# Causal mask of the turned attention scores: key-block rows in the stacks and zeroing on GpSimd, in place of mask products on TensorE

## The chip, the core and the metric

The kernel runs on one core of one Trainium2 chip. The core has TensorE (PE, matrix products; PEld is its weight load), VectorE (DVE), ScalarE (ACT), GpSimd (POOL), SyncE (SP, whose queue issues most DMAs), an on-chip memory of 128 partitions (SBUF) and eight accumulation banks (PSUM) that TensorE writes. Every engine works through its own queue in order, and the queues meet at semaphores. The metric is the time of one execution on the device in microseconds (us); lower is better.

## The reference

A transformer piece on x of shape 4 x 256 x 512 in fp32: causal attention with ALiBi, then a routed feed-forward (two of three experts), a gated MLP with a top-k cut, and the routed feed-forward again. The change lies in the attention:

```python
scores = jnp.einsum('bqhd,bkhd->bhqk', q, k) * SCALE      # 32 heads of 16, 4 batches of 256 tokens
rel = pos[None, :] - pos[:, None]
bias = slopes[:, None, None] * rel[None, :, :]
causal = rel <= 0
scores = jnp.where(causal[None, None], scores + bias[None], -jnp.inf)
attn = jax.nn.softmax(scores, axis=-1)
out = jnp.einsum('bhqk,bkhd->bqhd', attn, v).reshape(B, S, HIDDEN)
```

## The kernel before

**Stacks.** For every head, `qst` and `kst` hold queries and keys along partitions in bf16 parts: 96 rows of terms of q and k (`TROWS`), 8 rows of ALiBi parts (to `SROWS` = 104) and, for the turned scores alone, 3 rows that carry minus the maximum of each query (to `MROWS` = 107). One product of a stack of keys with a stack of queries so gives scores with bias, less the maximum.

**Stages.** Each of the four batches (b = 0 to 3) goes through projections, then scores with queries on partitions (`scores`, for the maxima that DVE reduces), then `attend`. In `attend` the scores are made again turned, with keys on partitions, in NG = 8 groups of G = 4 heads. The next batch's projections are woven into the score stage. After batch 3 come the feed-forward, the MLP and the second feed-forward, which the change leaves as they are.

**One group of `attend`, on each engine.** PE: `scores_t` (L1729 to L1749) writes three banks of slot g % 2. It first multiplies the identity with the mask `maskT` (L1737: 512 columns, L1740: twice 256), which puts -1e30 above the diagonal of the two square key/query tiles, and adds eight score products (L1744: 128 columns, L1746: 256 columns). ACT takes exp of all 1536 columns into `probsT` (L795), two buffers. PE `weigh` (L1756, L1761) multiplies the exponentials with the values. DVE copies the product out (`outT`, L1101), PE `back` (L1769) turns it, DVE divides (`normalise`: L1091, L1095, writes `o_tok`). `weigh(b, n)` waits for the exponentials of group n, and for `normalise` of group n-2, whose bank it takes. PE's order in step g is scores_t(g), weigh(g-1), back(g-2).

**What else stands on DVE's and POOL's queues in `attend`.** DVE: statistics of a normalisation (L1141) after groups 0 and 1, gate logits (`logit_row`, L1149, one after most groups of batches 1 and 2), the layer norm statistics of batch b+2 after group 3 (`ln_moments_of`) and its rows after group 5 (`ln_rows`, L1020), both for b < 2. In batch 3: three weight splits `w_first_lo` (L1351) ahead of group 0, and router steps of 4 to 14 tiny instructions after groups 2, 3, 5 and 6; ACT's exp of the router (L843) stands behind exp(3) and waits for the step after group 2. POOL: `norm_rstd` (L667, L670, L673) twice, and `ln` (L651, L653), on which DVE's `ln_rows` waits.

## Time and profile before

| | us |
|---|---|
| median of 3 runs (lowest, highest) | 714.89 (714.68, 716.71) |
| the profiled execution's own time | 714.72 |
| its span | 713.0 |
| PE busy in the span | 658.1 (92%) |
| DVE busy | 476.4 (67%) |
| ACT busy | 343.3 (48%) |
| POOL busy | 84.7 (12%) |
| exp L795, 32 of them | 46.2 busy, mean 1450 ns |

Starts are counted from the span's start. Matmuls overlap in PE's pipeline, so what a matmul costs is the distance to the next one's start, not its own duration. An entry in brackets behind a row is the idle time of the engine ahead of it and what ended it. The attend stages start at 68.2, 122.7, 178.2 and 225.7 us.

### The profile page before, as it was taken

The numbers are of one execution on the slowest core, as the hardware profiler recorded it, in microseconds if no ns is written. First come the engines' busy times: TensorE is split into PE (matmuls) and PEld (weight loads), VectorE is DVE, ScalarE is ACT, GpSimd is POOL, SyncE is SP. The second block draws the span as 40 slices with busy tenths as digits, with TensorE's granted clock in tenths as the row PEclk, the third lists the DMA queues.
The fourth block names the chain that finished last, engine by engine and source line by source line (L and its number), as shares of the span: only waits on it lengthen the run. The fifth ranks groups of instructions, "written<-read, shape, count | busy, mean of one in ns | idle before, by whom it ended". The sixth has DMA issues, their size and how long they took to land.

```text
span 713.0 us, 10154 instructions
## 1 busy us (share of the span) xinstructions
PE 658.1 (92%) x3784; PEld 486.1 (68%) x3784; DVE 476.4 (67%) x905; ACT 343.3 (48%) x536; POOL 84.7 (12%) x185
## 2 busy tenths in 40 slices
PE   5895999999998889999989999999999999999997
PEld 4783678678676567887776665756757555787875
DVE  6555495696589769787694655274463797868555
ACT  5221734613634663442357996485582924435221
POOL 4411002102100020100133000100100120100000
PEclk9987999999999999999999999999999999999999
DMA  8494423321744240000143000000001304000000
GB/s 269 123 276 123 116 63 89 94 90 56 236 124 151 106 151 9 0 1 1 25 169 126 0 1 0 1 0 1 0 1 42 136 0 177 2 29 16 16 30 30
DMA packets 31763, 51.35 MB, mean 72 GB/s; under 512 B 3433, under 2 KB 17132, under 8 KB 30159
## 3 DMA queue, kind: packets, MB, share of 16 engines
q1 hardware_dynamic: 31330, 49.12, 21.4%
q10 hardware_dynamic: 384, 1.57, 1.0%
q8 instruction: 31, 0.51, 0.3%
q14 instruction: 18, 0.15, 0.1%
HBM read 42.09 MB, written 8.40 MB: 71 GB/s over the span
## 4 chain that ended last, share of the span: by engine, by line
PE 76%; DVE 13%; ACT 4%; DMA 2%; issue 2%; POOL 1%; SPq 1%; ACTq 1%; DVEq 0%; POOLq 0%
PE ps L1815 12%; PE ps L1848 11%; PE ps L2040 11%; PE ps L1979 10%; PE ps L1678 6%; PE ps L1983 5%; PE ps L1756 2%; DVE nmax L1072 2%; PE ps L1746 2%; PE ps L1660 2%; PE ps L1824 2%; PE ps L1694 2%; DVE prodT L1587 1%; ACT sign_junk L966 1%; DVE x_sb L1416 1%
## 5 line engine op out<-in xcount | busy, mean ns | idle before, releaser
L2040 PE MATMUL ps<-wdT,prodT 128*128 128x512 f32 (+1 forms) x176 | 77.7, 597 | 0.4
L795 ACT ACTIVATE probsT<-ps 128x1536 f32<-128x1536 f32 x32 | 46.2, 1450 | 38.2 <-PE ps L1746 38.0
L2040 PEld LDWEIGHTS ps<-wdT,prodT 128*128 128x128 f32 (+1 forms) x176 | 32.8, 190 | 40.7 <-issue 38.3
L834 ACT ACTIVATE funs<-ps 128x512 f32<-128x512 f32 x16 | 9.6, 598 | 91.8 <-PE ps L1817 80.9
L667 POOL TENSOR_SCALAR ln_spread<-ln_moments 128x1 f32<-128x1 f32 x24 | 8.5, 354 | 298.4 <-DVE ln_moments L1143 298.3
L1149 DVE SCALAR_TENSOR_TENSOR junk<-x_sb,gate_row 128x512 f32<-128x512 f32 x48 | 41.2, 859 | 1.0
L1587 DVE COPY prodT<-ps 128x512 f32<-128x512 f32 (+1 forms) x24 | 13.7, 599 | 40.4 <-PE ps L2029 40.0
L1072 DVE TENSOR_REDUCE nmax<-ps 128x4 f32<-128x1024 f32 x32 | 38.8, 1213 | 0.0
L1416 DVE SCALAR_TENSOR_TENSOR x_sb<-b_row,coef,x_sb 128x512 f32<-128x512 f32 x48 | 36.2, 754 | 1.8
L901 ACT CAST aT_hi<-ps 128x512 fp32r<-128x512 f32 x32 | 17.2, 590 | 38.1 <-PE ps L1824 38.1
L966 ACT ACTIVATE sign_junk<-mlp_size_next,minus_guess 128x1376 bf16<-128x1376 f32 x24 | 34.6, 1443 | 0.8
L966 ACT ACTIVATE sign_junk<-mlp_size_main,minus_guess 128x1376 bf16<-128x1376 f32 x24 | 34.6, 1442 | 0.8
L1101 DVE COPY outT<-ps 128x256 f32<-128x256 f32 x32 | 13.5, 423 | 29.3 <-PE ps L1761 29.2
L660 POOL TENSOR_TENSOR parts<-resid,parts 128x512 bf16<-128x512 f32 x16 | 18.6, 1173 | 95.8 <-ACT parts L774 95.8
L1345 DVE TENSOR_TENSOR aT_lo<-ps,aT_hi 128x512 fp32r<-128x512 f32 x32 | 20.6, 685 | 12.8 <-ACT aT_hi L901 12.7
L1678 PE MATMUL ps<-rowsT_hi,wqkv_hi 128*128 128x256 f32 x128 | 23.6, 311 | 5.1 <-DVE rowsT_lo L1026 4.4
L1059 DVE SCALAR_TENSOR_TENSOR resid<-ps,qk_bias,parts 128x256 f32<-128x256 f32 x32 | 14.0, 479 | 18.3 <-ACT parts L767 18.3
L767 ACT ACTIVATE parts<-ps,qk_bias 128x256 bf16<-128x256 f32 x32 | 13.4, 468 | 26.7 <-PE ps L1678 26.6
L1425 DVE TENSOR_TENSOR x_sb<-ps,x_sb 128x512 f32<-128x512 f32 x16 | 11.0, 691 | 21.7 <-PE ps L1848 21.6
L1746 PE MATMUL ps<-qst,kst 107*128 107x256 bf16 x128 | 25.4, 278 | 0.0
L1717 PE MATMUL ps<-kst,qst 104*128 104x256 bf16 x128 | 24.5, 272 | 0.0
L1756 PE MATMUL ps<-probsT,v_ones 128*32 128x256 f32 x256 | 20.4, 391 | 3.9 <-DVE o_tok L1095 2.8
(280 smaller groups left out, 1720.5 us busy)
## 6 DMA issues: line engine op xcount, KB each, us to landing
cuts<-parts SPq DMA_DIRECT2D x16, 384.0 KB, 3.2
qst<-cuts SPq DMA_DIRECT2D x48, 128.0 KB, 2.7
w_first_raw<-in_L_ffn_w SPq DMA_DIRECT2D x6, 1024.0 KB, 8.0
w_second_raw<-in_L_ffn_w SPq DMA_DIRECT2D x6, 1024.0 KB, 8.6
kst<-cuts SPq DMA_DIRECT2D x36, 128.0 KB, 2.6
wqkv_raw<-in_L_attn_a_w_attn SPq DMA_DIRECT2D x3, 1024.0 KB, 8.2
wdT<-in_L_attn_b_w_down SPq DMA_DIRECT2D x1, 2560.0 KB, 10.0
wg_raw<-in_L_attn_b_w_gate SPq DMA_DIRECT2D x1, 2048.0 KB, 8.1
```

Of the source, the lines that this page charges most:

```text
L795: nc.scalar.activation(probsT[:, g % 2, :].rearrange("p (k n) -> p k n", k=3), slot[g % 2], ACT.Exp).then_inc(exp_ok.sem, 1)
L966: nc.scalar.activation(sign_junk[:, :], size_rows(n)[1][:, :], ACT.Sign, bias=minus_guess[:, i:i + 1], accum_out=probe_sum[:, i:i + 1]).th ...
L1072: nc.vector.tensor_reduce(nmax[:, 1, g * G:(g + 1) * G], sl[:, 1:3, :].rearrange("p s (h k) -> p (s h) k", h=2), AX.X, ALU.max, negate=Tru ...
L1149: nc.vector.scalar_tensor_tensor(out=junk[:, :], in0=x_sb[:, t, :], scalar=1.0, in1=gate_v[:, 0:D, e], op0=ALU.mult, op1=ALU.mult, accum_o ...
L1416: nc.vector.scalar_tensor_tensor(out=x, in0=b2_row[:, e, :], scalar=coef[:, n, e:e + 1], in1=x, op0=ALU.mult, op1=ALU.add).then_inc(ffn.b2 ...
L1678: last = nc.tensor.matmul(turn_bank(b, f)[:, m * S:(m + 1) * S], weight[:, side, c, columns], rows[:, c, :], start=(i == 0 and c == 0), st ...
L1746: m = nc.tensor.matmul(sl[:, 1 + i // 2, (i % 2) * S:(i % 2 + 1) * S], kst[0:MROWS, h, 0:P], qst[0:MROWS, h, :], start=False, stop=True, s ...
L1815: nc.tensor.matmul(ps[:, 2 * i + s, :], a[:, i, c, :], part[:, e, c, :], start=(k == 0 and c == 0), stop=False)
L1848: last = nc.tensor.matmul(ps[:, Y_BANK, :], a[:, s, c, :], part[:, e[s], c, :], start=(k == 0 and c == 0), stop=(k == len(products) - 1 an ...
L1979: last = nc.tensor.matmul(ps[:, first_bank + q, :], a[:, c, :], part[:, c, at_q], start=(k == 0 and c == 0), stop=(k == 2 and c == KC - 1))
L1983: last = nc.tensor.matmul(ps[:, first_bank + q, 0:IT], row_whole[:, c, :], end[:, c, :], start=(c == 0), stop=(c == KC - 1))
L2040: last = nc.tensor.matmul(ps[:, Y_BANK, :], prodT[0:m, c, :], wdT[0:m, c, :], start=(c == 0), stop=(c == IC - 1))
```

## The change

`maskT` and its three products are gone. The stacks get 15 more rows (`AROWS` = 122) for the turned scores: on the key side row i holds -1e30 for keys in a block of 16 behind block i, on the query side 1 for queries of block i. That masks keys of later blocks. Keys of the query's own block that lie behind the query are left, and POOL sets their exponentials to zero: `blank` does two `affine_select` per group, on 128 x 512 fp32 each, once exp has written them. `weigh` waits for POOL's count instead of ACT's, stands one group later in PE's order, and `probsT` has three buffers. The twice-per-batch `norm_rstd` and `ln` on POOL move behind groups 3, 4 and 6 of `blank`. Two DMAs bring the new rows (15 rows of 16 KB per stack) in the first stage. `h_sb`, `rowsT_lo` and `qk_bias` change places in SBUF.

```diff
 def alibi_rows(H, S):
...
+    q_rows += [0 * one] * MAX_PARTS
+    block = np.arange(S) // BLOCK
+    for i in range(S // BLOCK - 1):
+        k_rows.append(np.broadcast_to(bf16_parts(np.where(block > i, NEG, 0.0), 1)[0], (H, S)))
+        q_rows.append(np.broadcast_to(bf16_parts(np.where(block == i, 1.0, 0.0), 1)[0], (H, S)))
...
-        probsT = sb("probsT", [P, 2, 3 * D], F32)
+        probsT = sb("probsT", [P, 3, 3 * D], F32)
...
             gather(0, 1, (0,))
+            sp.dma_start(kst[MROWS:AROWS, :, :].bitcast(U16), k_alibi[MROWS - TROWS:]).then_inc(blocks_in, 16)
+            sp.dma_start(qst[MROWS:AROWS, :, :].bitcast(U16), q_alibi[MROWS - TROWS:]).then_inc(blocks_in, 16)
             sp.dma_start(x_sb[:, 2 * TB:T, :], x_v[:, 2 * TB:T, :]).then_inc(x_rest, 16)
...
+            def blank(b, between):
+
+                for g in range(NG):
+                    need(pool, exp_ok, b, g + 1)
+                    late = probsT[:, g % 3, 0:D].rearrange("p (h t) -> p h t", h=G)
+                    early = probsT[:, g % 3, D:].rearrange("p (h t) -> p h t", h=G)[:, :, 0:P]
+                    for weights in (early, late):
+                        nc.gpsimd.affine_select(out=weights, in_=weights, compare_op=ALU.is_ge, fill=0.0, base=0,
+                                                pattern=[[0, G], [1, P]], channel_multiplier=-1
+                                                ).then_inc(causal.sem, 1)
+                    between(g)
...
+            def small(b, g):
+                if b >= 1 and g in (3, 4):
+                    norm_rstd(norm2, (b - 1) * TB + g - 3)
+                if b + 2 < B and g == 6:
+                    ln(b + 2)
+
             for b in range(B - 1):
                 cut(b + 1)
-                if b >= 1:
-                    for j in range(TB):
-                        norm_rstd(norm2, (b - 1) * TB + j)
-                if b + 2 < B:
-                    ln(b + 2)
+                blank(b, lambda g: small(b, g))
             scale_route(norm2, route1, 0)
-            for t in range((B - 2) * TB, T):
+            blank(B - 1, lambda g: small(B - 1, g))
+            for t in range((B - 1) * TB, T):
                 norm_rstd(norm2, t)
...
-                    if g >= 2:
-                        need(act, pv_ps, b, g - 1)
-                    nc.scalar.activation(probsT[:, g % 2, :].rearrange("p (k n) -> p k n", k=3), slot[g % 2],
+                    if g >= 3:
+                        need(act, pv_ps, b, g - 2)
+                    nc.scalar.activation(probsT[:, g % 3, :].rearrange("p (k n) -> p k n", k=3), slot[g % 2],
...
-                nc.tensor.matmul(sl[:, 0, :].rearrange("p (h k) -> p h k", h=G), ident16[:, :], diagonal(maskT, G),
-                                 start=True, stop=False, skip_group_check=True)
-                for s in range(2):
-                    nc.tensor.matmul(sl[:, 1 + s, :].rearrange("p (h k) -> p h k", h=2)[:, :, 0:P], ident16[:, :],
-                                     diagonal(maskT, 2), start=True, stop=False, skip_group_check=True)
...
             def weigh(b, g):
-                need(pe, exp_ok, b, g + 1)
+                need(pe, causal, b, 2 * (g + 1))
...
-                for g in range(NG + 2):
+                for g in range(NG + 3):
                     if g < NG:
                         scores_t(b, g)
                     if g == 0 and 1 <= b < B - 1:
                         project_heads(b - 1, 1)
-                    if 1 <= g <= NG:
-                        n = g - 1
+                    if g == NG + 1 and b < B - 1:
+                        scores(b + 1, 0)
+                    if 2 <= g <= NG + 1:
+                        n = g - 2
...
                         weigh(b, n)
-                    if g == NG + 1 and b < B - 1:
-                        scores(b + 1, 0)
-                    if g >= 2:
-                        back(b, g - 2)
+                    if g >= 3:
+                        back(b, g - 3)
```

PE's queue in a middle group of batch 0, before. `ps` is PSUM; the first two lines are the mask products, L1744 and L1746 the score products (three more such pairs follow), L1756 and L1761 `weigh`, L1769 `back`.

```order
L1737 MATMUL ps<-maskT,ident_51 128x512 [waits exp_ok]
L1740 MATMUL ps<-maskT,ident_51 128x2x128 x2
L1744 MATMUL ps<-qst,kst 128x128
L1746 MATMUL ps<-qst,kst 128x256
...
L1756 MATMUL ps<-probsT,v_ones 32x256 [waits exp_ok,norm_ok]
L1756 MATMUL ps<-probsT,v_ones 32x256 x3
L1761 MATMUL ps<-probsT,v_ones 32x128 x4
L1769 MATMUL ps<-ident,outT 128x128 [waits outT_ok]
```

The same place in the changed kernel, whose line numbers are higher (L1760 and L1762 are the score products, L1772 and L1777 `weigh`, L1785 `back`):

```order
L1760 MATMUL ps<-qst,kst 128x128 [waits exp_ok]
L1762 MATMUL ps<-qst,kst 128x256
...
L1772 MATMUL ps<-probsT,v_ones 32x256 [waits causal,norm_ok]
L1772 MATMUL ps<-probsT,v_ones 32x256 x3
L1777 MATMUL ps<-probsT,v_ones 32x128 x4
L1785 MATMUL ps<-ident,outT 128x128 [waits outT_ok]
```

Three instructions are gone, and `weigh` waits for `causal`, which POOL raises, where it waited for `exp_ok`.

POOL's queue from the cuts of batches 0 and 1 (L660) over `ln` (L651, L653) to the first `norm_rstd`, in batch 1's attend stage, before:

```order
L660 TENSOR_TENSOR parts<-resid,parts 128x512 [waits part2] x8
L651 TENSOR_SCALAR spread<-moments 128x2 [waits stat]
L653 TENSOR_TENSOR rstd<-spread,neg_half 128x2 [waits rstd_ok]
L660 TENSOR_TENSOR parts<-resid,parts 128x512 [waits part2] x4
L667 TENSOR_SCALAR ln_spread<-ln_moments 128x1 [waits norm_stat]
L670 TENSOR_TENSOR ln_rstd<-ln_spread,neg_half 128x1 [waits norm_rstd]
L673 TENSOR_SCALAR ln_shift<-ln_moments,ln_rstd 128x1 [waits norm_rstd]
```

The changed kernel around group 3 of batch 1 (L677 is `affine_select`; `norm_rstd` is now L685, L688, L691):

```order
L677 AFFINE_SELECT probsT<-probsT 128x4x128 [waits exp_ok]
L677 AFFINE_SELECT probsT<-probsT 128x512
L685 TENSOR_SCALAR ln_spread<-ln_moments 128x1 [waits norm_stat]
L688 TENSOR_TENSOR ln_rstd<-ln_spread,neg_half 128x1 [waits norm_rstd]
L691 TENSOR_SCALAR ln_shift<-ln_moments,ln_rstd 128x1 [waits norm_rstd]
L677 AFFINE_SELECT probsT<-probsT 128x4x128 [waits exp_ok]
L677 AFFINE_SELECT probsT<-probsT 128x512
```

The three instructions of `norm_rstd` stood on a queue that nothing on PE waited for; now they stand between two groups' selects.

## Rows read from the trace of the kernel before

**Rows 1.** The page: span, and granted TensorE clock in 40 slices, in tenths.

```profile
span 713.0 us, 10154 instructions
...
PEclk9987999999999999999999999999999999999999
```

**Rows 2.** Timeline of PE, one group of batch 1: start, us, engine, line, operation.

```profile
131.04 0.38 PE L1737 MATMUL ps<-maskT,ident 128*128 128x512 bf16 x1
...
131.48 0.22 PE L1744 MATMUL ps<-qst,kst 107*128 107x128 bf16 x1
...
132.23 0.64 PE L1756 MATMUL ps<-probsT,v_ones 128*32 128x256 f32 x8
...
133.02 0.44 PE L1769 MATMUL ps<-ident,outT 128*128 128x128 f32 x2
133.30 0.38 PE L1737 MATMUL ps<-maskT,ident 128*128 128x512 bf16 x1
```

**Rows 3.** Timeline of ACT and DVE beside that group.

```profile
132.34 1.45 ACT L795 ACTIVATE probsT<-ps 128x1536 f32<-128x1536 f32 x1 [0.80 <-PE ps L1746]
...
133.16 0.42 DVE L1101 COPY outT<-ps 128x256 f32<-128x256 f32 x1 [0.56 <-PE ps L1761]
...
133.95 0.85 DVE L1149 SCALAR_TENSOR_TENSOR junk<-x_sb,gate_row 128x512 f32<-128x512 f32 x1
```

**Rows 4.** Timeline of PE, the end of batch 0's attend stage.

```profile
86.29 0.44 PE L1769 MATMUL ps<-ident,outT 128*128 128x128 f32 x2
87.35 0.64 PE L1756 MATMUL ps<-probsT,v_ones 128*32 128x256 f32 x8 [0.62 <-DVE o_tok L1095]
```

**Rows 5.** Timeline of POOL: selects and their nearest kin, and one `norm_rstd`.

```profile
8.96 0.95 POOL L630 MEMSET v_ones<- 128x1024 f32 x1
...
11.66 0.29 POOL L634 TENSOR_SCALAR_AFFINE_SELECT maskS<-maskS 128x128 bf16<-128x128 bf16 x1
...
12.66 0.45 POOL L643 TENSOR_TENSOR text<-ones,vision 128x128 f32<-128x128 f32 x1
...
111.01 1.16 POOL L660 TENSOR_TENSOR parts<-resid,parts 128x512 bf16<-128x512 f32 x1 [27.89 <-ACT parts L774]
...
130.25 0.23 POOL L667 TENSOR_SCALAR ln_spread<-ln_moments 128x1 f32<-128x1 f32 x1 [8.12 <-DVE ln_moments L1143]
...
131.24 0.27 POOL L673 TENSOR_SCALAR ln_shift<-ln_moments,ln_rstd 128x1 f32<-128x1 f32 x1
```

**Rows 6.** Timeline of POOL ahead of the MLP.

```profile
372.49 1.73 POOL L716 TENSOR_TENSOR hT_lo<-hT_all,hT_hi 128x512 fp32r<-128x512 f32 x1 [5.43 <-ACT hT_all L941]
374.18 2.28 POOL L716 TENSOR_TENSOR hT_lo_third<-hT_all_third,hT_hi_third 128x512 fp32r<-128x512 f32 x1
```

**Rows 7.** Timeline of DVE in the same stretch, and just behind it.

```profile
373.10 2.21 DVE L1600 TENSOR_TENSOR wu_lo<-wu_raw,wu_hi 128x1024 fp32r<-128x1024 f32 x1
...
377.05 1.22 DVE L1600 TENSOR_TENSOR wu_lo<-wu_raw,wu_hi 128x1024 fp32r<-128x1024 f32 x1
```

**Rows 8.** Timeline: attend of batch 0, first product and first of the next stage.

```profile
68.24 0.61 PE L1737 MATMUL ps<-maskT,ident 128*128 128x512 bf16 x1 [3.84 <-DMA qst<-nmaxT]
...
89.65 1.17 PE L1660 MATMUL ps<-wqkv_hi,rowsT_hi 128*128 128x512 f32 x4
```

**Rows 9.** Timeline: attend of batch 1, PE's first product, DVE's first reduction behind it.

```profile
122.67 0.39 PE L1737 MATMUL ps<-maskT,ident 128*128 128x512 bf16 x1 [1.42 <-DMA qst<-nmaxT]
...
147.79 0.69 DVE L1069 TENSOR_REDUCE nmax<-ps 128x4 f32<-128x512 f32 x1
```

**Rows 10.** Timeline: attend of batch 3, PE, DVE and ACT.

```profile
225.74 0.39 PE L1737 MATMUL ps<-maskT,ident 128*128 128x512 bf16 x1 [0.75 <-DMA qst<-nmaxT]
...
247.70 1.09 PE L1685 MATMUL ps<-ident,o_tok 128*128 128x128 f32 x8 [1.18 <-DVE o_tok L1095]
...
227.07 2.28 DVE L1351 TENSOR_TENSOR w_first_lo<-w_first_raw,w_first_hi 128x2048 fp32r<-128x2048 f32 x1
...
236.28 0.21 ACT L843 ACTIVATE tiny<-tiny 128x12 f32<-128x12 f32 x1 [1.84 <-DVE tiny L1283]
```

More of the change, by code:

```diff
@@ L25 @@
 MAX_PARTS = 3
+BLOCK = 16
 FIRST_GUESS = 0.78
@@ L181, in build @@
     MROWS = SROWS + MAX_PARTS
+    AROWS = MROWS + S // BLOCK - 1
     SCALE = 1.0 / HD
@@ L281, in build @@
         wqkv_lo = sb("wqkv_lo", [P, 3, KC, D], F32R, wqkv_at)
-        qk_bias = sb("qk_bias", [P, 2, HT], F32)
-        at[0] = wqkv_at + 3 * 4 * KC * D + 4 * TB * 2 * D
+        h_sb = sb("h_sb", [P, TB, D], F32)
+        rowsT_lo = sb("rowsT_lo", [P, KC, S], F32R)
         parts = sb("parts", [P, 2, 2, 3, HT // 2, S], BF16)
@@ L302, in build @@
         maskS = sb("maskS", [P, P], BF16)
-        maskT = sb("maskT", [P, P], BF16)
+        qk_bias = sb("qk_bias", [P, 2, HT], F32)
         nmax = sb("nmax", [P, TB, H], F32)
@@ L307, in build @@
         nmaxT = sb("nmaxT", [P, S], BF16)
-        h_sb = sb("h_sb", [P, TB, D], F32)
         stats = sb("stats", [P, TB, 6], F32)
@@ L389, in build @@
         wqkv_in = [sem(f"wqkv_in{n}") for n in range(3)]
-        wproj_in, alibi_in, bias_in = sem("wproj_in"), sem("alibi_in"), sem("bias_in")
+        wproj_in, alibi_in, blocks_in, bias_in = sem("wproj_in"), sem("alibi_in"), sem("blocks_in"), sem("bias_in")
         consts, ident_ok, bits_set = sem("consts"), sem("ident_ok"), sem("bits_set")
@@ L421, in build @@
         exp_ok = sig("exp_ok", NG)
+        causal = sig("causal", 2 * NG)
         pv_ps = sig("pv_ps", NG)
@@ L526, in _ @@
             sp.dma_start(bias_v[:, :], b_attn[2 * D:3 * D].partition_broadcast(P)).then_inc(bias_v_in, 16)
-            sp.dma_start(kst[TROWS:MROWS, :, :].bitcast(U16), k_alibi).then_inc(alibi_in, 16)
-            sp.dma_start(qst[TROWS:SROWS, :, :].bitcast(U16), q_alibi).then_inc(alibi_in, 16)
+            sp.dma_start(kst[TROWS:MROWS, :, :].bitcast(U16), k_alibi[0:MROWS - TROWS]).then_inc(alibi_in, 16)
+            sp.dma_start(qst[TROWS:SROWS, :, :].bitcast(U16), q_alibi[0:SROWS - TROWS]).then_inc(alibi_in, 16)
             sp.wait_ge(bias_cut, 4)
@@ L622, in constants @@
                 nc.gpsimd.memset(maskS[:, :], 0.0).then_inc(consts, 1)
-                nc.gpsimd.memset(maskT[:, :], 0.0).then_inc(consts, 1)
                 nc.gpsimd.memset(vision[:, :], 1.0).then_inc(consts, 1)
@@ L632, in constants @@
                 nc.gpsimd.tensor_copy(ident16[:, :], ident[:, :]).then_inc(consts, 1)
-                pool.wait_ge(consts, 5)
+                pool.wait_ge(consts, 4)
                 nc.gpsimd.affine_select(out=maskS[:, :], in_=maskS[:, :], compare_op=ALU.is_ge, fill=NEG,
                                         base=0, pattern=[[-1, P]], channel_multiplier=1).then_inc(consts, 1)
-                nc.gpsimd.affine_select(out=maskT[:, :], in_=maskT[:, :], compare_op=ALU.is_ge, fill=NEG,
-                                        base=0, pattern=[[1, P]], channel_multiplier=-1).then_inc(consts, 1)
                 nc.gpsimd.affine_select(out=vision[:, :], in_=vision[:, :], compare_op=ALU.is_ge, fill=0.0,
@@ L641, in constants @@
                                         base=0, pattern=[[0, P]], channel_multiplier=-1).then_inc(consts, 1)
-                pool.wait_ge(consts, 10)
+                pool.wait_ge(consts, 8)
                 nc.gpsimd.tensor_tensor(text[:, :], ones32[:, :], vision[:, :], ALU.subtract).then_inc(consts, 1)
@@ L1736, in scores_t @@
                     need(pe, exp_ok, b, g - 1)
-                nc.tensor.matmul(sl[:, 0, :].rearrange("p (h k) -> p h k", h=G), ident16[:, :], diagonal(maskT, G),
-                                 start=True, stop=False, skip_group_check=True)
-                for s in range(2):
-                    nc.tensor.matmul(sl[:, 1 + s, :].rearrange("p (h k) -> p h k", h=2)[:, :, 0:P], ident16[:, :],
-                                     diagonal(maskT, 2), start=True, stop=False, skip_group_check=True)
                 for i in range(G):
                     h = g * G + i
-                    nc.tensor.matmul(sl[:, 0, i * P:(i + 1) * P], kst[0:MROWS, h, P:S],
-                                     qst[0:MROWS, h, P:S], start=False, stop=True, skip_group_check=True)
+                    nc.tensor.matmul(sl[:, 0, i * P:(i + 1) * P], kst[0:AROWS, h, P:S],
+                                     qst[0:AROWS, h, P:S], start=True, stop=True, skip_group_check=True)
                     m = nc.tensor.matmul(sl[:, 1 + i // 2, (i % 2) * S:(i % 2 + 1) * S],
-                                         kst[0:MROWS, h, 0:P], qst[0:MROWS, h, :],
-                                         start=False, stop=True, skip_group_check=True)
+                                         kst[0:AROWS, h, 0:P], qst[0:AROWS, h, :],
+                                         start=True, stop=True, skip_group_check=True)
                 m.then_inc(sT_ps.sem, 1)
             def weigh(b, g):
-                need(pe, exp_ok, b, g + 1)
+                need(pe, causal, b, 2 * (g + 1))
                 o_ps = work[g % 2]
@@ L1873, in attend @@
                 need(pe, nm_in, b, nm_in.per)
+                if b == 0:
+                    pe.wait_ge(blocks_in, 32)
                 need(pe, v_out, b, TB)
-                for g in range(NG + 2):
+                for g in range(NG + 3):
                     if g < NG:
@@ L1904, in _ @@
             pe.wait_ge(alibi_in, 32)
-            pe.wait_ge(consts, 11)
+            pe.wait_ge(consts, 9)
             scores(0, 0)
```

5 lines of the change are left out of this document (2 added, 3 removed).

## Prediction

> **What bounds the kernel now.** I read the page first: a span of 713.0 us [rows 1], in which PE is busy 92%. Then PE's timeline through the attend stages, where the change lies. A middle group takes 133.30 - 131.04 = 2.26 us, and no row of it has a wait: masks 131.48 - 131.04 = 0.44, score products and a gap of 0.09 to 132.23 = 0.75, weigh 0.79, back 0.28 [rows 2]. ACT works 1.45 of it and idles 0.80 [rows 3]. So PE bounds a group. The next limit is close. DVE's loop, from the end of one weigh to the start of the next, shows at the stage's end, where no scores stand between: weigh ends at 86.29, the next starts at 87.35 behind `o_tok`, 1.06 us [rows 4]. With the 0.79 of weigh itself a group cannot go below 1.85 us; PE alone would reach 2.26 - 0.44 = 1.82.
>
> **What is removed.** 32 groups x 0.44 us of mask products, 14 us of PE. Of a middle group only 2.26 - 1.85 = 0.41 can be kept, and only where nothing else on DVE, ACT or POOL ends later. The 15 more rows cost nothing on PE: the columns that stream are the same. The two DMAs of 240 KB and the constants lie under the first stage's projections, 20 us ahead of their use; I cost them at 0, and if that cover failed they would cost the transfer of half a megabyte, some 3 us.
>
> **What is added: the select.** The trace has a select on 128 columns only: 0.29 us [rows 5]. Bounds for 512 columns. Below: the memset's rate, at most 0.95 us / 1024 = 0.93 ns per column, with no fixed part is 512 x 0.93 = 0.48; I walk this end with 0.52. Above: the rate of two-input work on POOL, (1.16 - 0.45) / 384 = 1.85 ns per column, gives 0.29 + 0.71 = 1.0, or 0.95 where neighbours overlap a little. Outermost: four times 0.29 = 1.16. Between them 0.29 + 384 x 0.93 ns = 0.65, less the overlap. A select reads one input, so its nearest row is the memset's and not the two-input one: I take 0.60, 1.2 us per group. POOL alone then keeps up with 1.85 easily.
>
> The Trainium skill, page "GPSIMD Engine Reference", section "Performance pitfalls for Q7 kernels", gives compare-and-select loops 2.03 cycles per element, and 1.03 when unrolled by two. As an estimate from that page, the two rates would make the select about 0.9 or 0.6 us; no row here has a select long enough to tell which.
>
> **What is added: a shared resource.** `wu_lo` (both inputs in SBUF) takes 1.22 us by itself and 2.21 where POOL is inside `hT_lo`: its start at 373.10 is pushed to where POOL's 372.49 + 1.73 ends. POOL's next, 374.18, stands beside `wu_lo` and takes 2.28 where the same operation took 1.73 just before [rows 6, 7]. So I read that such DVE instructions and POOL's exclude each other, each waiting for the other's current one. What DVE reads from PSUM I take as free of it. In attend the excluded ones are `logit_row` (0.85 [rows 3]), `ln_rows`, the weight splits and the router's tiny steps. Before, POOL did some 3 us per stage; now it does 10 to 13, in the middle of DVE's loop.
>
> **The stages, by a walk.** I put each queue's instructions in order with their durations (scores 0.66, weigh 0.79, back 0.28, exp 1.35 to 1.45; outT, reciprocal and o_tok together 133.95 - 133.16 = 0.79 [rows 3]; handovers of 0.1 to 0.2, such as 133.02 to 133.16) and start each when its queue, its semaphores and, for the excluded, the other engine are free. On before's queues this gives 20.4, 25.2 (to DVE's end), 23.0 and 22.0 us for batches 0 to 3; the rows have 89.65 - 68.24 = 21.4 [rows 8], 147.79 - 122.67 = 25.1 [rows 9] and 247.70 - 225.74 = 22.0 [rows 10]. Only batch 0 is off, by the first three microseconds, in which PE runs at the lower of its two clocks (granted clock 0.7 on average in that slice [rows 1], behind an idle time of 3.84 us [rows 8]).
>
> Batch 0. scores(0) ends at 0.66, exp(0) at 2.3, and scores(2), which now stands ahead of weigh(0), waits for it. Selects 2.39 to 3.59, weigh(0) 3.69. Then steps of 1.54 and three of 1.84; 2.29 behind DVE's statistics after group 3; 1.84; 2.73, because `ln_rows` waits for POOL's `ln`, which now stands behind select(6), and for select(7). weigh(7) starts at 17.61 and the next stage at 19.45: 0.95 less than 20.4. Two groups' masks at the lower clock would have cost 0.4 more. **Gain 1.35.**
>
> Batch 1. Head projections cover the start: weigh(0) at 5.17, then 2.28, 1.84, 1.84. `norm_rstd` costs POOL 131.51 - 130.25 = 1.26 us [rows 5] after groups 3 and 4 each, and a logit row excludes POOL after most groups: steps of 2.29, 2.42, 2.05, and 3.94 to weigh(7), where `ln`, two rows of `ln_rows` and selects take turns. DVE ends at 26.55 against 25.23, and its end is what starts the next maxima (no idle time ahead of 147.79 [rows 9]). **Loss 1.3.**
>
> Batch 2. Six logit rows, no `ln`: weigh(5) comes 4.1 behind weigh(4), the rest is near 1.85. End 23.48 against 22.96. **Loss 0.5.**
>
> Batch 3. First, exp(0) is done at 2.4, but `w_first_lo` runs from 1.3 to 3.5 (227.07 + 2.28 against 225.74 [rows 10]) and excludes the select: weigh(0) at 4.8 instead of 2.8. Second, ACT's exp of the router waits already 1.84 us for DVE's router step [rows 10]; that step follows weigh(2), which now stands behind scores(4). It ends at 12.1, ACT's exp(4) starts at 12.25 instead of 10.64, and all behind it: weigh(4) 15.25 instead of 12.17. Third, select and tiny router steps take turns to the end: `o_tok` of group 7 is done at 26.8 instead of 22.0. **Loss 4.8.**
>
> **Sum.** 1.35 - 1.3 - 0.5 - 4.8 = -5.3. The profiled execution's own time is 714.72, 0.17 below the median of the runs shown. 714.72 + 5.3 = **720.0 us**. Behind batch 3 I let the delay through in full: PE, ACT and DVE hang on each other there. With selects of 0.52 the same walk gives 1.8, -0.5, 0 and -3.9, so 717.3; with 0.75 it loses 11.0 (725.7), with 0.95 it gives -1.5, -5.9, -4.3 and -9.5, so 736.
>
> **Rivals.**
>
> *A, no exclusion.* The selects do not collide with DVE: the walk without it, at 0.60, gives 1.8, 1.15, 2.0 and -1.45, together 3.5, so **711.2**, faster. For it: no row shows a select beside a two-input instruction of DVE, and the logit rows may fall between selects. Against: rows 6 and 7, both ways. It decides on the step from exp to weigh: if a select beside a logit row takes 0.6 and not 1.4, this is the case.
>
> *B, the select costs at the two-input rate,* 0.95: POOL needs 1.9 a group plus its waits and bounds every stage: **736**. For it: the fp32 tile is computed element by element against an index pattern with two dimensions, one of the tiles with gaps. Against: 0.29 for 128 columns against 0.45 of the two-input kind. The slower of the two rates of the Trainium skill, "GPSIMD Engine Reference", "Performance pitfalls for Q7 kernels", would lead to this case.
>
> *C, it evens out.* Exclusion holds, but the tiny router steps slip between selects and the stall of batch 3 is 1.5 rather than 4.8, while batches 1 and 2 are even: about 1.35 - 1.5, so **715**.
>
> *D, the change doesn't do what it says:* the scores keep their wait elsewhere and masks gone from PE change nothing, since ACT (1.45 a group) or DVE's loop take their place. In batch 0 that would be steps of 2.2 instead of 1.85. I see nothing for it, and fold it into C.
>
> **How the numbers follow.** Forecast (exclusion, select 0.52 to 0.8): 0.60. A: 0.19. B: 0.08. C and D: 0.13. A measurement of this kernel can tell some 0.3%, 2.1 us, from no change. Faster: A and a little of C, 0.21. Same: most of C and the fast edge of the forecast, 0.13. Slower: 0.66. The range reaches down to A's time, 711, and up to a select of 0.8, 728, which leaves out most of B and A's faster half; the forecast's own range is 716.5 to 727.
>
> **What would show it.** In the profile after: the selects' row, near 600 ns, and 1.2 to 1.5 where a logit row or a weight split of DVE lies beside; PE's step from weigh to weigh 1.85 in batch 0; the idle time of PE ahead of weigh put down to POOL in batches 1 to 3; ACT idle ahead of the router's exp over 4 us; attend stages near 20.1, 26.5, 23.5 and 26.8 us. The forecast is wrong if batches 1 and 2 are shorter than before (then A), if steps in batch 0 exceed 2.2 (then B), or if batch 3 is under 23.5 us.

## The result, and the profile after

The changed kernel takes 720.88 us (median of 8 executions, 718.63 to 723.04), the kernel before beside it 715.82: ratio 1.0067, 95% interval 1.0044 to 1.009. It is slower by 0.7%; 720.0 was forecast. The profiled execution took 722.62 of its own time, 1.7 above the median, so the trace shows a little more loss than there is on average.

The page of the changed kernel, to be held against [rows 1]:

```profile
span 720.9 us, 10022 instructions
...
PE 654.2 (91%) x3688; PEld 480.6 (67%) x3688; DVE 478.8 (66%) x905; ACT 342.5 (48%) x536; POOL 125.4 (17%) x247
...
PEclk9987999999999989999999999999999999999999
...
PE 71%; DVE 13%; ACT 5%; POOL 4%; issue 3%; DMA 2%; SPq 1%; ACTq 1%; POOLq 0%; DVEq 0%
...
L677 POOL TENSOR_SCALAR_AFFINE_SELECT probsT<-probsT 128x512 f32<-128x512 f32 x64 | 42.3, 688 | 57.0 <-ACT probsT L816 56.3
```

PE lost only 3.9 us of its 658.1 busy us, though 14 us of mask products are gone: most of the rest was handed back in products at a lower clock (mean granted clock 0.971 over the span, 0.983 before; run 2 below, without the masks and at 0.981, has PE busy for 645.8 us). POOL now has 4% of the chain, 1% before, and PE waits 5.9 us for its selects in the attend stages, where it did not wait for POOL before. The fifteenth digit of the clock, 252 to 270 us, is an 8 where it was a 9; shorter falls don't show in slices of 18 us.

Steps from weigh to weigh in batch 0, where the group of before took 2.26 us [rows 2]:

```profile
72.84 0.64 PE L1772 MATMUL ps<-probsT,v_ones 128*32 128x256 f32 x8 [0.38 <-POOL probsT L677]
...
74.39 0.64 PE L1772 MATMUL ps<-probsT,v_ones 128*32 128x256 f32 x8
...
76.24 0.64 PE L1772 MATMUL ps<-probsT,v_ones 128*32 128x256 f32 x8
...
78.10 0.64 PE L1772 MATMUL ps<-probsT,v_ones 128*32 128x256 f32 x8
```

They are 1.85 us apart, DVE's loop as forecast. The bounds of the four stages, first products on PE and what followed, the counterparts of [rows 8 to 10]:

```profile
68.44 0.29 PE L1760 MATMUL ps<-qst,kst 122*128 122x128 bf16 x1 [3.84 <-DMA qst<-nmaxT]
...
88.22 1.16 PE L1681 MATMUL ps<-wqkv_hi,rowsT_hi 128*128 128x512 f32 x4
...
121.26 0.23 PE L1760 MATMUL ps<-qst,kst 122*128 122x128 bf16 x1 [1.42 <-DMA qst<-nmaxT]
...
146.97 0.68 DVE L1090 TENSOR_REDUCE nmax<-ps 128x4 f32<-128x512 f32 x1
...
228.45 0.23 PE L1760 MATMUL ps<-qst,kst 122*128 122x128 bf16 x1 [1.36 <-DMA qst<-nmaxT]
...
253.71 1.97 PE L1706 MATMUL ps<-ident,o_tok 128*128 128x128 f32 x8 [1.21 <-DVE o_tok L1116]
```

Batch 0 takes 88.22 - 68.44 = 19.8 us against 21.4, batch 1 25.7 against 25.1, batch 3 25.3 against 22.0. Batch 2 takes 25.6 against 22.7, by these rows, of the changed kernel and of the kernel before:

```profile
177.38 0.23 PE L1760 MATMUL ps<-qst,kst 122*128 122x128 bf16 x1 [1.43 <-DMA qst<-nmaxT]
...
202.98 1.19 PE L1681 MATMUL ps<-wqkv_hi,rowsT_hi 128*128 128x512 f32 x4
```

```profile
178.19 0.39 PE L1737 MATMUL ps<-maskT,ident 128*128 128x512 bf16 x1 [1.42 <-DMA qst<-nmaxT]
...
200.91 1.17 PE L1660 MATMUL ps<-wqkv_hi,rowsT_hi 128*128 128x512 f32 x4
```

For a common measure of all kernels below I use one number per stage: us from the stage's first product on PE (a mask product in the kernels that have them there) to the start of the last weigh (of group 7), from PE's timeline, each in its profiled execution. "To there" is the time from the span's start to batch 3's last weigh, "rest" what follows to the end of the span.

| kernel | batch 0 | 1 | 2 | 3 | to there | rest | median, ratio to before (95%) |
|---|---|---|---|---|---|---|---|
| before | 19.1 | 20.4 | 20.4 | 18.9 | 244.6 | 468.4 | |
| changed | 17.9 | 21.1 | 23.4 | 22.2 | 250.7 | 470.3 | 720.9, 1.0067 (1.0044-1.0090) |
| no selects | 17.6 | 18.7 | 18.4 | 20.1 | 239.7 | 473.4 | 712.3, 0.9923 (0.9897-0.9949) |
| no selects, old order | 17.2 | 18.3 | 17.3 | 17.2 | 237.0 | 469.8 | 708.1, 0.9880 (0.9844-0.9916) |
| masks, later order | 20.2 | 21.5 | 21.5 | 21.1 | 249.2 | 473.1 | 720.9, 1.0051 (1.0029-1.0072) |
| selects, old order | 23.2 | 23.4 | 24.4 | 25.5 | 265.7 | 471.5 | 737.3, 1.0274 (1.0237-1.0310) |
| logit rows of one input | 18.7 | 19.7 | 19.1 | 22.4 | 245.2 | 470.0 | 717.0, 0.9991 (0.9970-1.0012) |
| selects aside | 17.6 | 21.9 | 18.4 | 20.1 | 243.7 | 470.0 | 719.7, 1.0037 (1.0006-1.0068) |
| masks and selects | 20.4 | 22.4 | 21.8 | 23.1 | 252.7 | 470.0 | 724.0, 1.0103 (1.0066-1.0140) |
| `ln` early | 18.3 | 20.8 | 20.6 | 23.2 | 249.0 | 471.5 | 719.7, 1.0053 (1.0032-1.0073) |
| batches 0 to 2 | 17.8 | 21.1 | 21.1 | 18.9 | 244.2 | 469.4 | 717.6, 1.0023 (1.0005-1.0041) |
| batch 0 alone | 18.5 | 20.4 | 20.4 | 18.9 | 244.2 | 469.8 | 714.3, 0.9963 (0.9939-0.9988) |
| batch 0, `ln` early | 18.8 | 20.4 | 20.4 | 18.9 | 244.0 | 468.3 | 714.0, 0.9976 (0.9962-0.9991) |
| batches 0 and 1, `ln` early | 18.5 | 20.8 | 20.4 | 18.9 | 244.0 | 469.2 | 714.7, 0.9984 (0.9968-1.0000) |

Two things about its use. Batches 1 to 3 with the masks and the old order repeat to 0.1 us from kernel to kernel. Changed stages do not always: batch 0, which begins at a lower clock and ends with rows of `h_sb` among the selects, lies between 17.8 and 18.7 with the same code, batch 2 took 23.4 in one trace and 21.1 in another (run 9), and batch 3 22.2 and 23.2 (run 7); where batches 2 and 3 differ so, the granted clock does too. The rest does not repeat, since TensorE's granted clock falls for a while in other places of it each time. And the executions of one kernel differ: those of the kernel before ran from 714.57 us (granted clock 0.986) to 720.47 (0.979) in one set. So mechanisms are read from the stages, verdicts from the ratios (the kernel before was run again beside each set of four, with medians of 717.44, 717.25 and 715.19, so the medians of different sets cannot be compared as they are).

### The profile page after: what moved, and what is told of

The parts are those of the page before. It is cut to its first block, busy times and chain, and to the rows that moved or that the text cites. A ratio compares the mean times of both kernels' runs of the same rounds, so it can differ in the third digit from the quotient of the medians.

```text
span 720.9 us, 10022 instructions
## 1 busy us (share of the span) xinstructions
PE 654.2 (91%) x3688; PEld 480.6 (67%) x3688; DVE 478.8 (66%) x905; ACT 342.5 (48%) x536; POOL 125.4 (17%) x247
## 3 DMA queue, kind: packets, MB, share of 16 engines
q1 hardware_dynamic: 31390, 49.61, 21.9%
## 4 chain that ended last, share of the span: by engine, by line
PE 71%; DVE 13%; ACT 5%; POOL 4%; issue 3%; DMA 2%; SPq 1%; ACTq 1%; POOLq 0%; DVEq 0%
PE ps L1831 12%; PE ps L1864 11%; PE ps L2058 11%; PE ps L1997 10%; PE ps L1699 6%; PE ps L2001 5%; POOL probsT L677 2%; DVE nmax L1093 2%; PE ps L1681 2%; PE ps L1840 2%; PE ps L1715 2%; DVE prodT L1608 1%; PE ps L1772 1%; ACT sign_junk L987 1%; DMA qst<-nmaxT 1%
## 5 line engine op out<-in xcount | busy, mean ns | idle before, releaser
L677 POOL TENSOR_SCALAR_AFFINE_SELECT probsT<-probsT 128x512 f32<-128x512 f32 x64 | 42.3, 688 | 57.0 <-ACT probsT L816 56.3
L685 POOL TENSOR_SCALAR ln_spread<-ln_moments 128x1 f32<-128x1 f32 x24 | 9.5, 398 | 243.4 <-DVE ln_moments L1164 242.9
L922 ACT CAST aT_hi<-ps 128x512 fp32r<-128x512 f32 x32 | 17.2, 590 | 37.2 <-PE ps L1840 37.2
L1760 PE MATMUL ps<-qst,kst 122*128 122x128 bf16 x128 | 24.6, 230 | 11.3 <-DMA qst<-nmaxT 8.0
L1772 PE MATMUL ps<-probsT,v_ones 128*32 128x256 f32 x256 | 21.8, 412 | 11.2 <-POOL probsT L677 5.9
L1366 DVE TENSOR_TENSOR aT_lo<-ps,aT_hi 128x512 fp32r<-128x512 f32 x32 | 20.6, 685 | 12.8 <-ACT aT_hi L922 12.7
L1080 DVE SCALAR_TENSOR_TENSOR resid<-ps,qk_bias,parts 128x256 f32<-128x256 f32 x32 | 14.0, 479 | 18.9 <-ACT parts L788 18.9
L1762 PE MATMUL ps<-qst,kst 122*128 122x256 bf16 x128 | 26.1, 287 | 0.0
```

The costliest lines, as they stand in the source:

```text
L677: nc.gpsimd.affine_select(out=weights, in_=weights, compare_op=ALU.is_ge, fill=0.0, base=0, pattern=[[0, G], [1, P]], channel_multiplier=- ...
```

## The experiments

**1. The selects taken out.**

```diff
-                    for weights in (early, late):
-                        nc.gpsimd.affine_select(out=weights, in_=weights, compare_op=ALU.is_ge, fill=0.0, base=0,
...
-                need(pe, causal, b, 2 * (g + 1))
+                need(pe, exp_ok, b, g + 1)
```

> The changed kernel without the selects on GpSimd (the mask inside a query's own block of 16 keys is left out); weigh waits for the exp of its group, order and buffers stay. Theory (the selects, and what they share with DVE's instructions, cost the time; the later order costs some of batch 3): attend stages 19.4, 24.2, 22.0, 22.9 us against 19.8, 25.7, 25.6, 25.3, no stretch of a lower granted clock in batches 2 and 3 or behind them, so 711 to 712. Rival (the order and the third buffer are at fault, not the selects): 718 to 720. Rival (the removed masks leave TensorE idle and its clock falls whatever POOL does): batch 2 stays at 24 to 25 and the time at 716.

Measured: 712.31 us, just above the theory's 711 to 712; ratio 0.9923; the stages as in the table. The selects, with all that they set off, cost about 1.4% (0.9923 against 1.0067), some 10 us: more than the masks' removal can bring. Batch 3 stays at 20.1, above the 18.9 of before: that part is not POOL's. The lower clock came here too, in the middle of batch 3 (0.92 over 220 to 242 us), so "no stretch of a lower granted clock" was wrong.

**2. Values one group behind the scores again, without selects.** As run 1, and in PE's queue:

```diff
-                for g in range(NG + 3):
+                for g in range(NG + 2):
...
-                    if 2 <= g <= NG + 1:
-                        n = g - 2
+                    if 1 <= g <= NG:
+                        n = g - 1
```

> As the run without selects, but values one group behind the scores again. Theory (the later order costs a group's scores at the start of each stage and, in batch 3, at the router's step): first weigh of a stage 0.7 us sooner, the router's exp and all behind it 1 to 1.5 us sooner, last weighs at 17.2, 18.2, 17.9, 18.5 us (17.6, 18.7, 18.4, 20.1 with the later order); 709 to 711. Rival (with shorter scores the later order is needed for the steps of 1.85 even without selects): steps of 2.0 to 2.2, 714 to 716.

Measured: 708.06, ratio 0.9880, stages 17.2, 18.3, 17.3, 17.2, so a little under the expected 709 to 711, since batch 3 came 1.3 us sooner than expected. The rival is out: steps of 1.85 need no later order when nothing stands between exp and weigh. This is the worth of the masks' removal, 1.2% (the mask inside a block of 16 keys is left out here too). The 15 rows, the third buffer, the two DMAs and the tiles' new places are all in this run, so they are not what makes the changed kernel slow. ACT's exp of the router, the counterpart of [rows 10], first in run 1 and then here:

```profile
229.60 0.21 ACT L858 ACTIVATE tiny<-tiny 128x12 f32<-128x12 f32 x1 [3.59 <-DVE tiny L1298]
```

```profile
229.06 0.21 ACT L858 ACTIVATE tiny<-tiny 128x12 f32<-128x12 f32 x1 [1.87 <-DVE tiny L1298]
```

1.87 us of waiting is the 1.84 of before; the changed kernel waits 3.68 and run 1, without any select, 3.59. The wait that the order adds in batch 3 comes from the order alone. Behind it PE waits for that group's exp, again run 1 first:

```profile
231.21 0.23 PE L1754 MATMUL ps<-qst,kst 122*128 122x128 bf16 x1 [1.92 <-ACT probsT L810]
```

```profile
230.76 0.64 PE L1766 MATMUL ps<-probsT,v_ones 128*32 128x256 f32 x8 [1.35 <-ACT probsT L810]
```

The granted clock over 231 to 238 us is 0.76 in run 1 and 1.00 here, and run 1 takes 5.2 us from weigh(4) to weigh(6) where this run takes 3.7. So of the 2.9 us between the two batches 3 about 1.5 lie in steps at a lower clock, and 1.3 are the order's own: 0.67 at weigh(0) and 0.67 at the router's step. In batches 0 to 2 the later last weigh costs next to nothing, since the next batch's scores stand ahead of it: from batch 0's start to batch 3's it is 151.3 us in run 1 and 151.1 here.

**3. The later order with the mask products, without selects,** on the kernel before (diff as in run 2, reversed, three buffers, and the changed kernel's places in SBUF).

> The kernel before with its mask products, and only the order of the change (values two groups behind the scores, three buffers), no select. Theory: PE stays the bound of a group at 2.26 us, so batches 0 to 2 keep 21.4, 25.1 and 22.7; in batch 3 the router's step of DVE stands behind weigh(2), which stands behind scores(4), so ACT waits longer ahead of the router's exp (3 us and more instead of 1.84) and the stage takes 23.3 instead of 22.0: 716 to 717. Rival (order is free): 714.7 to 715.8.

Measured: 720.91, ratio 1.0051, more than expected. Batch 3 lost 2.2 us where 1.3 were expected (it takes 24.2 us, not 23.3), with the wait ahead of the router's exp at 4.08. What was not said: in each of the others the first weigh comes 1.1 us later (5.05 instead of 4.00 in batch 0, 6.42 instead of 5.32 in 1 and 2), because scores(2) with its masks stands ahead of it, and the steps stay 2.25. From the start of one stage to the next, 0.6 to 1.0 us of it remain. The order is a cost in itself, and the selects are why it is there, as the next run shows.

**4. Selects, but the old order** (run 2's diff on the changed kernel).

> The changed kernel with the order alone undone: selects, but values one group behind the scores. Theory: exp, two selects and their handovers (1.5 + 1.35) stand between scores(g) and weigh(g), with scores(g+1) alone beside them, so a pair of groups takes 0.79 + 0.94 + 2.9 = 4.6 us, steps of 2.3 instead of 1.85: last weighs of batches 0 to 3 at 20.5, 22.5, 23, 24 us, 725 to 728. Rival (the order is worth nothing here, DVE's loop sets the steps anyway): 718 to 720.

Measured: 737.30, ratio 1.0274. PE in batch 0:

```profile
78.80 0.64 PE L1772 MATMUL ps<-probsT,v_ones 128*32 128x256 f32 x8 [1.05 <-POOL probsT L677]
...
80.68 0.64 PE L1772 MATMUL ps<-probsT,v_ones 128*32 128x256 f32 x8
...
83.62 0.64 PE L1772 MATMUL ps<-probsT,v_ones 128*32 128x256 f32 x8 [1.05 <-POOL probsT L677]
```

A pair of groups takes 83.62 - 78.80 = 4.82 (4.6 expected): exp, two selects and weigh stand in one chain. With selects the later order is worth 2% (1.0274 against 1.0067). Without them it costs 0.4% by runs 1 and 2, whose intervals overlap, and 0.5% by run 3, whose interval is clear of no change. The time is 9 us above the expected range: PE waits 26.9 us for POOL in 18 waits, and from 240 to 268 us it has a granted clock of 0.88.

**5. Gate logits with one input in SBUF.**

```diff
+                if route is route1 and t < (B - 1) * TB - 1:
+                    nc.vector.tensor_reduce(logits[:, t, e:e + 1], x_sb[:, t, :], AX.X, ALU.add
+                                            ).then_inc(route.logit.sem, 1)
+                    return
```

> The changed kernel; for tiles 0 to 6 the gate logit is a plain sum of the row (one input in SBUF; the product with the gate's column is left out), selects as they are. Theory of exclusion between a select and a DVE instruction with two inputs in SBUF: the pairs of selects of 1.9 us beside such a row go back to 1.22, batch 1 from 25.7 to 24.8, batch 2 from 25.6 to 23 (the idle time behind which the clock falls goes), batch 3 unchanged but for less of the low clock: 716 to 718. Rival (a select is slowed by any instruction of DVE, or it is the time of the selects alone): pairs stay at 1.9 and the time at 720 to 721.

The edit reaches tiles 0 to 4 and not 0 to 6, which takes in every logit row that stands in batches 1 and 2.

Measured: 717.01, ratio 0.9991, in the theory's 716 to 718 (the stages went lower than it said, to 23.7 and 21.0 us in batches 1 and 2). POOL beside a logit row, first in the changed kernel, then in this run, at the same place of batch 2, with DVE's rows of the changed kernel between:

```profile
188.52 1.91 POOL L677 TENSOR_SCALAR_AFFINE_SELECT probsT<-probsT 128x512 f32<-128x512 f32 x2
190.51 0.74 POOL L685 TENSOR_SCALAR ln_spread<-ln_moments 128x1 f32<-128x1 f32 x1
```

```profile
188.39 0.93 DVE L1170 SCALAR_TENSOR_TENSOR junk<-x_sb,gate_row 128x512 f32<-128x512 f32 x1
...
190.24 0.92 DVE L1170 SCALAR_TENSOR_TENSOR junk<-x_sb,gate_row 128x512 f32<-128x512 f32 x1
...
192.29 1.30 DVE L1170 SCALAR_TENSOR_TENSOR junk<-x_sb,gate_row 128x512 f32<-128x512 f32 x1
```

```profile
187.67 1.23 POOL L677 TENSOR_SCALAR_AFFINE_SELECT probsT<-probsT 128x512 f32<-128x512 f32 x2
188.98 0.22 POOL L685 TENSOR_SCALAR ln_spread<-ln_moments 128x1 f32<-128x1 f32 x1
```

The pair starts inside the row and takes 1.91, 0.68 more than beside a row with one input, and even a POOL instruction on one column, begun inside the row of 190.24, takes 0.74 instead of 0.22. The other way round DVE's row at 192.29, begun beside selects, takes 1.30 instead of 0.86. Batches 1 and 2 come down by 1.5 and 4.2 us; of the latter 2.3 is clock (below). The rows show the exclusion; how much of the time it costs they do not separate. A sum takes 0.68 where a logit row takes 0.86, and it has no second instruction to read the accumulator (0.09), so each of the six rows in a stage is 0.3 shorter, together up to 1.6 us, as much as the whole remainder. Against that being all of it stands run 1, which keeps the long rows and has its last weighs at 18.7 and 18.4. The Trainium skill, page "SBUF — State Buffer", section "Who interferes with whom", says that a DVE instruction with two SBUF inputs contends with a GpSimd instruction that reads SBUF, that the contention is an exclusive lock, and that the order of issue decides who blocks; both directions in these rows agree.

**6. Selects aside.** They work on a tile that nobody reads, and batch 3 has none (that edit, the tile's memset and the wait ahead of its later DMA are left out here):

```diff
-                    for weights in (early, late):
-                        nc.gpsimd.affine_select(out=weights, in_=weights, compare_op=ALU.is_ge, fill=0.0, base=0,
+                    for k in range(2):
+                        need(pool, causal, b, 2 * g + k)
+                        nc.gpsimd.affine_select(out=b2_row[:, 1, :].rearrange("p (h t) -> p h t", h=G),
+                                                in_=b2_row[:, 1, :].rearrange("p (h t) -> p h t", h=G),
...
-                need(pe, causal, b, 2 * (g + 1))
+                need(pe, exp_ok, b, g + 1)
```

> The changed kernel with the selects of batches 0 to 2 at the same points of GpSimd's queue but on a 2 KB tile of its own that nobody reads, weigh waiting for exp alone; none in batch 3. (The mask inside a query's own block of keys is left out.) Theory: weigh's wait for POOL is most of the loss, DVE's logit rows stretched to 1.3 us and its rows of the first norm are a smaller part: last weighs of batches 0 to 2 at 17.9, 19.5 and 19.0 us (without selects 17.6, 18.7, 18.4; changed kernel 17.9, 21.1, 23.4), so 712 to 714. Rival (the loss comes through DVE, whose instructions the selects hold up): 20.5 and over in batches 1 and 2, 716 to 718.

Measured: 719.66, ratio 1.0037 (714.98 to 724.60, clock 0.978 to 0.960): the theory's 712 to 714 is out, and the rival's mechanism is not it either. The trace is of one of the shorter executions (715.42) and splits by batch. In batches 0 and 2 there is no loss at all (17.6 and 18.4, as without selects): there the collisions alone cost the stage nothing, and what the changed kernel loses beyond its clock goes through weigh's wait for the selects. In batch 1 there is one place, DVE and behind it PE:

```profile
140.71 1.61 DVE L1046 TENSOR_SCALAR h_sb<-x_sb,moments,rstd 128x512 f32<-128x512 f32 x2 [3.03 <-POOL rstd L661]
```

```profile
143.15 0.64 PE L1777 MATMUL ps<-probsT,v_ones 128*32 128x256 f32 x8 [3.10 <-DVE o_tok L1121]
...
145.07 2.07 PE L1686 MATMUL ps<-wqkv_hi,rowsT_hi 128*128 128x512 f32 x4
```

`ln` stands behind select(6) in POOL's queue, POOL is late, and DVE's in-order queue stops for it: 3.03 us, against 1.06 in the changed kernel. The two rows of `h_sb` then take 1.61 beside selects; in the kernel before, at the same place of batch 1, they take 0.99:

```profile
140.71 0.99 DVE L1020 TENSOR_SCALAR h_sb<-x_sb,moments,rstd 128x512 f32<-128x512 f32 x2
```

PE idles 3.10, and after it four products take 2.07 that took 1.16 above (granted clock 0.74 over 145 to 150 us). That the other executions, longer and at still lower clocks, lose it in the same place is likely, but no trace shows them, so 4.2 us of the median, 719.66 against 715.42, are without a shown cause.

**7. `ln` earlier** in POOL's queue, `norm_rstd` later:

```diff
-                if b >= 1 and g in (3, 4):
-                    norm_rstd(norm2, (b - 1) * TB + g - 3)
-                if b + 2 < B and g == 6:
-                    ln(b + 2)
+                last = b == B - 1
+                if b + 2 < B and g == 5:
+                    ln(b + 2)
+                if b >= 1 and g in ((3, 4) if last else (6, 7)):
+                    norm_rstd(norm2, (b - 1) * TB + g - (3 if last else 6))
```

> The changed kernel; in GpSimd's queue of batches 0 to 2 the statistics of the first norm (ln) stand behind the selects of group 5 instead of 6, and norm_rstd behind those of groups 6 and 7 instead of 3 and 4. Theory (the loss of batch 1 comes from DVE waiting for ln and from rows of h_sb and selects that hold each other up): last weigh of batch 0 at 17.6 instead of 17.9, of batch 1 at 19.7 instead of 21.1, batch 2 22 to 23: about 2 us less than the changed kernel, 718 to 719. Rival (the selects beside the logit rows are the loss, the place of ln is not): 720 to 721.

Measured: 719.71, ratio 1.0053 (changed kernel 1.0067; the intervals overlap). Batch 1 gained 0.3 of the 1.4 us expected; batch 0 shows nothing beyond its spread. That what a place in POOL's queue gives to DVE is taken from the selects behind it is my reading; no run separates it. Batch 3, whose code is the changed kernel's, took 23.2 here with a granted clock of 0.83 over 225 to 235 us.

**8. Mask products back, beside the selects** (the diff of the change's three products, reversed).

> The changed kernel with the mask products put back beside the selects: TensorE gets 0.44 us more to do in each of 32 groups, and POOL and DVE have what the change gave them. Theory (in batches 1 to 3 the selects and DVE set the pace, and the clock falls only because TensorE idles): the last weigh of the stages comes at 20.4, 22, 22.5, 23.5 us after the first scores, no stretch of 0.74 in 190 to 200, together 2 to 4 us more than the changed kernel: 722 to 725. Rival (TensorE's products still count in full): 14 us x 0.41/0.44 more, 732 to 734.

Measured: 723.98, ratio 1.0103, inside the theory's 722 to 725 and far from the rival's 732. 14 us of PE work, put back, cost 0.4% or 3 us by the ratios, whose intervals overlap; 14 us would be 2%, far outside them. In batches 1 to 3 they lie in gaps: PE waits for POOL 1.8 us in total instead of 5.9, and batch 2 is even shorter than in the changed kernel's trace (21.8 against 23.4), at a granted clock of 1.00.

**9. Batches 0 to 2 changed, batch 3 as before.** `SELECTED` names the batches that are changed; the others have the masks and the old order:

```diff
+SELECTED = (0, 1, 2)
...
+                fresh = b in SELECTED
...
+                lag = 2 if b in SELECTED else 1
+                for g in range(NG + lag + 1):
```

> The change in batches 0 to 2, batch 3 with mask products and values one group behind as before. Theory: batch 3's last weigh goes back from 22.2 to 18.9 and nothing else moves, so 3.3 us less than the changed kernel, 717 to 718, more if TensorE's clock also stays up behind it. Rival (batch 3's loss was the clock, which falls anyway behind batch 2): 720.

Measured: 717.56, ratio 1.0023. Batch 3's last weigh is back at 18.9, and the ratio fell by 0.0044, 3.2 us: batch 3's loss is its own. This run also prices the clock in batch 2. PE there, first in the changed kernel:

```profile
194.24 0.66 PE L1772 MATMUL ps<-probsT,v_ones 128*32 128x256 f32 x8 [1.77 <-POOL probsT L677]
...
196.56 1.08 PE L1772 MATMUL ps<-probsT,v_ones 128*32 128x256 f32 x8 [0.62 <-DVE o_tok L1116]
197.42 0.66 PE L1777 MATMUL ps<-probsT,v_ones 128*32 128x128 f32 x8
198.00 0.69 PE L1785 MATMUL ps<-ident,outT 128*128 128x128 f32 x2
```

and in this run:

```profile
194.45 0.64 PE L1792 MATMUL ps<-probsT,v_ones 128*32 128x256 f32 x8 [1.83 <-POOL probsT L686]
...
196.31 0.64 PE L1792 MATMUL ps<-probsT,v_ones 128*32 128x256 f32 x8 [0.63 <-DVE o_tok L1125]
196.76 0.40 PE L1797 MATMUL ps<-probsT,v_ones 128*32 128x128 f32 x8
```

The same waits, 1.77 and 1.83, then 0.62 and 0.63; behind them one runs at the lower level (1.2 GHz; granted clock 0.74 over 190 to 200 us) and the other at the upper one (1.00). The last weigh comes at 23.4 in one and 21.1 in the other: 2.3 us of clock. The whole stage takes 200.41 - 177.44 = 23.0 us here, 0.3 more than before.

**10. Batch 0 alone,** `SELECTED = (0,)`.

> The change in batch 0 alone (15 more rows, selects, values two groups behind); batches 1 to 3 with mask products and values one group behind, as before. Theory: batch 0 gains its 1.6 us, nothing is lost later: 714.2, 1.6 below the kernel before. Rival (the gain of batch 0 is given back by what follows it, the clock or the handover to batch 1): 715.8.

Measured: 714.28, ratio 0.9963 (0.9939 to 0.9988), so it beats both kernels. The median is the theory's 714.2, but the kernel before beside it was at 717.44 and not at the 715.8 from which that was reckoned, and the trace shows less than 1.6 us: batch 1 starts 53.4 us behind batch 0 instead of 54.4, and batch 3's last weigh comes 0.5 sooner. The gain is shown, its size of 1.6 is not.

**11 and 12. The same with `ln` early, and with batch 1 too** (`SELECTED = (0, 1)`).

> The change in batch 0 alone, with ln behind the selects of group 5. Theory: last weigh of batch 0 at 17.6 to 17.9 instead of 18.5, 0.6 to 0.9 less than with the change in batch 0 alone: 713.5. Rival (DVE comes to the rows of h_sb no sooner): 714.3.

> The change in batches 0 and 1, with ln behind the selects of group 5 and norm_rstd behind those of 6 and 7; batches 2 and 3 as before. Theory: batch 1's last weigh at 19.7 against 20.4 with masks, so 0.5 us less than the same in batch 0 alone: 713. Rival (batch 1 loses to selects beside logit rows whatever stands where, and idle TensorE lowers its clock): 714.5 to 716.

Measured: 714.01, ratio 0.9976, and 714.70, ratio 0.9984. The first expectation stays undecided: its median is 0.3 lower, its ratio 0.13% higher, and the intervals overlap. In its trace the second weigh comes at 6.94 instead of 5.96, so that the last is at 18.8; why was not followed up. Batch 1 in the new way has its last weigh at 20.8, 0.4 later than with masks, and the time lies in the rival's range: the trace says that batch 1 is better left as it was, though the ratios of the two runs overlap.

## Why the prediction was right, and where not

**Direction and size.** Forecast +5.3 us, measured +5.1 between the medians (3 to 6 by the interval of the ratio); the profiled pair differs by 7.9. The 720.0 started from 714.72, and the kernel before has a median of 715.82 in eight executions. As the sum had it, with what the two traces show: batch 0 +1.35, measured +1.6; batch 1 -1.3, measured -0.6; batch 2 -0.5, measured -2.9; batch 3 -4.8, measured -3.3; outside the four stages 0, measured -2.8 (1.9 of it behind batch 3). So the total agrees partly by luck: batches 1 and 3 were forecast too dear, and a loss of 2 to 5 us was not in the sum. Batch 2 was right but for the clock: run 9, with the same code at the upper level, loses 0.3 there where 0.5 was forecast.

**The select** was sized right: 0.61 us in a pair (1.23 for two), 0.60 taken. Rival B is out. The faster of the two rates of the Trainium skill, "GPSIMD Engine Reference", "Performance pitfalls for Q7 kernels", whose estimate was 0.6, is the one that agrees.

**The exclusion** is there (run 5), so A fails as a mechanism, and its 711.2 is out of reach: the kernel takes 712.3 even without any select. But its price was put too high. Where a POOL instruction and a row meet, one of the two takes some 0.4 to 0.8 us more. In batch 1 I had put 3.94 us on the step to weigh(7); it took 3.45 (21.13 - 17.68).

**The order** was priced only in batch 3, beyond a later weigh(0) in the walk. That holds: by runs 2 and 1 (0.9880 to 0.9923, 0.4% or 3 us) batch 3 has 2.9 us, of which 1.3 are the order's waits and 1.5 the lower clock behind them, and the last weighs of the others, 0.4 to 1.1 later, delay the next stages by 0.2 in all.

**Batch 3,** its three parts. The weight split: weigh(0) forecast at 4.8, it came at 4.2, at 3.1 without selects; a collision (the first select takes 1.10 us beside the split), smaller than thought, since the split began 0.7 us into the stage and not 1.3. The router's exp behind the later order: forecast wait over 4 us, measured 3.68, and the runs tie it to the order alone. The turns of selects and tiny router steps: these fail. Of some thirty steps in the trace two are stretched, to 0.55 and 0.62 from under 0.25; the others find room between selects, since POOL is idle while ACT waits. C had said so, and put batch 3's stall at 1.5; the truth, 3.3, lies between. Part of that 3.3 is clock, which fell here in run 1 too; how much was not separated in the changed kernel.

**The chain of the gain** was what the table gives: masks gone, -7.6 us to the last weigh (237.0 against 244.6); the later order, +2.7; the selects, +10.9 in the profiled execution, 2.3 of them clock in batch 2.

**What the prediction did not have** is TensorE's clock. I used its fall only for the first microseconds of batch 0 and took 1.00 for the rest. The waits that the selects and the later order put into batches 2 and 3 leave PE idle, and the clock fell there and behind batch 3. Granted clock by stretch:

```profile
177.00:203.00 26.00, 22.23 (x233) 0.87 0.75 232
203.00:228.00 25.00, 22.39 (x145) 1.00 0.13 45
228.00:254.00 26.00, 17.86 (x214) 0.91 0.43 153
254.00:262.00 8.00, 8.00 (x28) 0.65 0.01 2
```

(Columns: stretch, its length, PE busy, granted clock, DMA share and rate.) The eight turns of `o_tok` at 253.71 take 1.97 where they took 1.09 in [rows 10]. Yet the runs with the same waits show it in one execution and not in another (run 9), and run 1, without selects, lost more in the rest (473.4) than the changed kernel. So the part in batch 2 and in the rest comes in some executions and not in others, and its mean I can give only from the ratios: batches 0 to 2 changed cost 0.23% where the stages alone (244.2) would have given 0.4 us back. In batch 3 the traces agree more, though there is one of each kernel: PE's wait for the exp behind the router's was 1.92 to 1.93 us in the changed kernel and runs 1, 5, 6 and 7, and the clock fell beside it in all five; it was 0.52 to 1.52 before and in runs 2, 3 and 8, and the clock stayed at 1.00. What exactly makes the clock fall stays open.

## What to carry to other kernels

An engine that gets a step between producer and consumer costs more than the step: here it needed a later order (a pair of groups took 4.82 us without it), which delays whatever else hangs on that order, here a router's step behind a weigh. Before moving work to GpSimd, count for each stage the VectorE instructions with two SBUF inputs beside it, and those that, like the rows of `h_sb`, took longer beside selects with one; the stage that has few (batch 0: the two rows of `h_sb`) is where the change paid, and it can be made there alone. And price a removed product on a nearly full engine by the next loop (1.85 us), not by its length: here 14 us of products were worth 9 at the best, and 3 once others set the pace.
